# One strip for the last key tile of four heads, and values projected in 64-column pieces, in a fused cross-attention and expert-FFN kernel

## The reference

```
x = x + attention(layernorm(x), ctx)
x = x + experts(layernorm(x))
```

```
q = x @ Wq ;  k, v = split(concat(ctx, x) @ Wkv)
dots = q k^T * scale ;  masked where  key index > query index + 154
out = softmax(dots) v ;  out @ Wout + bout
```

## Time and profile before

| | |
|---|---|
| median of three runs | 375.83 us (374.93 to 376.63) |
| the profiled execution, its own time | 376.98 us |
| its span, first to last instruction | 375.2 us |
| PE busy | 352.5 us (94%), 4336 matmuls |
| ACT busy | 266.3 us (71%), 385 instructions |
| DVE busy | 211.8 us (56%), 724 instructions |
| POOL busy | 117.9 us (31%), 178 instructions |
| mean granted clock of PE | 0.971 of 2.4 GHz |

### The profile page before, as it was taken

The page is one execution under the profiler, slowest core; times in us unless marked ns, Lnnn a source line. Parts: engine busy times, 40 slices in busy tenths (PEclk is TensorE's granted clock), DMA queues, the critical chain, the costliest instruction groups (busy, mean ns, idle before and its releaser), DMA issues.

```text
span 375.2 us, 10982 instructions
## 1 busy us (share of the span) xinstructions
PE 352.5 (94%) x4336; PEld 228.0 (61%) x4336; DVE 211.8 (56%) x724; ACT 266.3 (71%) x385; POOL 117.9 (31%) x178
## 2 busy tenths in 40 slices
PE   8999999899999999999999999996858999999993
PEld 7757547343544444443534445585747899999992
DVE  4999698353637455563737445398778332323231
ACT  2675563899999999999999999614871545454630
POOL 5445775000004030300304030601431646464522
PEclk9999999899999999999999999999795999999999
DMA  7733799500538435553449513800660522322100
GB/s 245 199 111 116 247 238 312 183 6 3 140 108 271 122 101 139 155 140 96 119 130 260 126 36 63 279 0 2 224 226 3 146 88 65 106 73 92 59 26 31
DMA packets 37325, 47.68 MB, mean 127 GB/s; under 512 B 8764, under 2 KB 26610, under 8 KB 37265
## 3 DMA queue, kind: packets, MB, share of 16 engines
q1 hardware_dynamic: 34368, 40.26, 36.8%
q0 software_dynamic: 2560, 6.30, 5.6%
q10 hardware_dynamic: 337, 0.32, 0.3%
HBM read 32.71 MB, written 13.81 MB: 124 GB/s over the span
## 4 chain that ended last, share of the span: by engine, by line
PE 76%; DVE 10%; ACT 9%; issue 2%; POOL 2%; POOLq 0%
PE ps L1116 18%; PE ps L1092 16%; PE ps L1297 10%; PE ps L1309 9%; PE ps L1077 8%; ACT pbuf L858 8%; PE ps L1029 5%; DVE pbuf L1632 4%; PE ps L1230 3%; PE ps L999 1%; DVE stats L1666 1%; DVE xe L1661 1%; PE ps L1286 1%; PE ps L1178 1%; POOL pbuf L754 1%
## 5 line engine op out<-in xcount | busy, mean ns | idle before, releaser
L858 ACT ACTIVATE pbuf<-ps 128x1024 f32<-128x1024 f32 (+3 forms) x192 | 169.4, 1028 | 3.2 <-PE ps L1092 3.0
L1632 DVE SCALAR_TENSOR_TENSOR pbuf<-pbuf,seen 128x128 f32<-128x128 f32 (+2 forms) x288 | 76.4, 307 | 65.5 <-ACT pbuf L858 64.5
L1092 PE MATMUL ps<-q_st,k_st 98*32 98x512 bf16 (+4 forms) x2048 | 102.0, 319 | 2.8 <-ACT pbuf L858 2.6
L1116 PE MATMUL ps<-pbuf,v_st 128*32 128x512 f32 (+4 forms) x1024 | 98.0, 478 | 1.9 <-DVE pbuf L1632 1.9
L1092 PEld LDWEIGHTS ps<-q_st,k_st 98*32 98x32 bf16 x2048 | 51.8, 96 | 69.8 <-issue 28.1
L726 POOL TENSOR_TENSOR mid<-mid 64x256 f32<-64x256 f32 x28 | 20.5, 763 | 120.9 <-DMA mid<-reciprocals 120.9
L1116 PEld LDWEIGHTS ps<-pbuf,v_st 128*32 128x32 f32 x1024 | 27.5, 110 | 26.9 <-issue 11.8
L1297 PEld LDWEIGHTS ps<-mid,piece_f 128*128 128x128 f32 x320 | 38.7, 192 | 1.6 <-issue 0.7
L1297 PE MATMUL ps<-mid,piece_f 128*128 128x128 f32 x320 | 39.0, 275 | 0.5 <-issue 0.5
L1309 PE MATMUL ps<-pbuf,mid 128*128 128x256 f32 x160 | 37.7, 380 | 0.0
L940 ACT ACTIVATE mid<-ps 128x512 f32<-128x512 f32 x20 | 11.9, 597 | 34.4 <-PE ps L1297 34.3
(11 more groups left out here) (253 smaller groups left out, 370.2 us busy)
## 6 DMA issues: line engine op xcount, KB each, us to landing
wts<-in_L_ffn_W SPq DMA_DIRECT2D x16, 512.0 KB, 5.0
k_st<-k_cut SPq DMA_DIRECT2D x48, 147.2 KB, 3.0
q_st<-q_cut SPq DMA_DIRECT2D x48, 128.0 KB, 2.9
q_cut<-wts SPq DMA_DIRECT2D x8, 384.0 KB, 3.4
k_cut<-wts SPq DMA_DIRECT2D x8, 384.0 KB, 3.9
token_rows<-xe SPq DMA_DIRECT2D x4, 512.0 KB, 4.2
mid<-mid SPq DMA_DIRECT2D x28, 64.0 KB, 2.6
mid<-reciprocals SPq DMA_DIRECT2D x28, 64.0 KB, 2.3
```

The source lines that it names most:

```text
L858: nc.scalar.activation(pbuf[:, s % 2, r, c0:c1], st_ps[(s * GH + r) % NST][:, c0:c1], ACT.Exp, scale=SCALE).then_inc(exp_done, 1)
L1092: last = nc.tensor.matmul(st_ps[(s * GH + r) % NST][c:c + 32, a:z], k_st[pa][:, r, t * P + c:t * P + c + 32], q_st[pa][:, r, q0 + a - c0:q ...
L1116: last = nc.tensor.matmul(o_ps[32 * r:32 * r + 32, a:z], v_st[pa][:, t, r, :], pbuf[:, s % 2, r, a + dc:z + dc], start=(t == 0), stop=(t = ...
L1632: last = nc.vector.scalar_tensor_tensor(a, a, 3.0e38, seen[:, off:off + w], ALU.min, ALU.mult)
```

## The change

Tile 9 of the four heads shares one strip of `pbuf` and of PSUM. Head `h`'s 26 keys take the partitions 32h to 32h+25 of the tile's 26 columns in the slot of head 3. So

- `scores` leaves tile 9 out for heads 0 to 2 and makes for head 3 four matmuls, one for each head's keys and queries, one in each column group;
- `exps` ends 26 columns earlier (948 instead of 974) for heads 0 to 2 in step 3;
- `masks` handles tile 9 once, for head 3, with a mask `seen_short` that holds the corner of `seen` four times, one below the other, made by four more copies in `order_constants`;
- `values` reads the strip for all four heads. `v_st` of tile 9 keeps 128 rows, and head r's columns are zero outside its 32 rows; the column of ones is set by four small memsets a buffer instead of one;
- the value job that holds tile 9 projects the tile's first 32 rows (26 keys and 6 of padding) into each of the four partition groups, with the 64 columns of one head of each group of heads, so eight matmuls of 64 columns stand for two of 256;
- `load_v` makes four small copies of 32 rows by 16 columns, each waited for, then the copy of the nine other tiles, waited for too. Ahead of piece 15 it also waits for `low_done` of the pieces before.

```diff
--- before.py
+++ after.py
@@ -107,6 +107,9 @@
 
 
 LAST = NB * NG - 1
+SHORT = JT - 1
+SHORT_KEYS = J - SHORT * P
+assert SHORT_KEYS <= 32 and GH == 4 and any(len(tiles) > 1 and tiles[-1] == SHORT for tiles in STEP_TILES)
 
 
 def xattn_ffn(nc, x, ctx, Wq, Wkv, Wout, bout, Wg, W1, W2, out, rows_d, qd, kd, sums_d, recs_d, force_shift=False):
@@ -208,6 +211,7 @@
         before = sb("before", [P, P], BF16)
         ones_b = sb("ones_b", [P, P], BF16)
         seen = sb("seen", [P, P])
+        seen_short = sb("seen_short", [P, 32])
         irow = sb("irow", [P, 1], I32)
         ir2 = sb("ir2", [P, 1], I32)
         fcol = sb("fcol", [P, P])
@@ -281,6 +285,7 @@
         ones_rows = sem("ones_rows")
         rows_sent = sem("rows_sent")
         v_in = sem("v_in")
+        short_in = sem("short_in")
         biased = sem("biased")
         st_ready = sem("st_ready")
         exp_done = sem("exp_done")
@@ -687,8 +692,9 @@
                 made += 1
             pool.wait_ge(st_made, made)
             for i in range(2):
-                nc.gpsimd.memset(v_st[i][0:J - (JT - 1) * P, JT - 1, :, HD:HD + 1], 1.0).then_inc(st_made, 1)
-                made += 1
+                for r in range(GH):
+                    nc.gpsimd.memset(v_st[i][32 * r:32 * r + SHORT_KEYS, SHORT, r, HD:HD + 1], 1.0).then_inc(st_made, 1)
+                    made += 1
             pool.wait_ge(st_made, made)
             nc.gpsimd.memset(tri[:, :], 0.0).then_inc(tri_made, 1)
             pool.wait_ge(tri_made, 1)
@@ -697,15 +703,21 @@
 
             def load_v(pa, b, m):
                 g = 2 * m + pa
-                nc.gpsimd.tensor_copy(v_st[pa][:, :, :, 0:HD],
-                                      v_all[:, bass.ds(b, 1), :, bass.ds(g * (GH * HD), GH * HD)]
-                                      .rearrange("p b t (h c) -> p (b t) h c", h=GH)).then_inc(v_in, 1)
+                for r in range(GH):
+                    nc.gpsimd.tensor_copy(v_st[pa][32 * r:32 * r + 32, SHORT, r, 0:HD],
+                                          v_all[32 * r:32 * r + 32, b, SHORT, (g * GH + r) * HD:(g * GH + r + 1) * HD]).then_inc(short_in, 1)
+                    pool.wait_ge(short_in, (b * NG + g) * GH + r + 1)
+                nc.gpsimd.tensor_copy(v_st[pa][:, 0:SHORT, :, 0:HD],
+                                      v_all[:, b, 0:SHORT, g * (GH * HD):(g + 1) * (GH * HD)]
+                                      .rearrange("p t (h c) -> p t h c", h=GH)).then_inc(v_in, 1)
+                pool.wait_ge(v_in, b * NG + g + 1)
 
 
             for i in range(len(QK)):
                 w = JOBS[QK[i]][4]
                 if i == PER_B + 5:
                     pool.wait_ge(vcopy_done, len(VJ) // 2)
+                    pool.wait_ge(low_done, i)
                     for pa in range(2):
                         load_v(pa, 0, 0)
                 pool.wait_ge(lo_done, i + 1)
@@ -851,11 +863,12 @@
                     c0 = STEPS[s][0][2]
                     c1 = STEPS[s][-1][2] + S - STEPS[s][-1][1]
                     for r in range(GH):
+                        end = c1 - SHORT_KEYS if STEPS[s][-1][0] == SHORT and r < GH - 1 else c1
                         act.wait_ge(st_ready, (g0 * NSTEP + s) * GH + r + 1)
                         if r == 0:
 
                             act.wait_ge(pv_done, g0 * NSTEP + s + 1)
-                        nc.scalar.activation(pbuf[:, s % 2, r, c0:c1], st_ps[(s * GH + r) % NST][:, c0:c1], ACT.Exp,
+                        nc.scalar.activation(pbuf[:, s % 2, r, c0:end], st_ps[(s * GH + r) % NST][:, c0:end], ACT.Exp,
                                              scale=SCALE).then_inc(exp_done, 1)
 
             for g in range(2 * NG):
@@ -1026,8 +1039,15 @@
                     pe.wait_ge(tr_done, flipped(b, (t + 2) * P))
                     for i in range(2):
                         for k in range(KT):
-                            last = nc.tensor.matmul(bk[:, i * D:(i + 1) * D], xcT[:, b, k, (t + i) * P:(t + i + 1) * P],
-                                                    wkv_sb[:, k, D:2 * D], start=(k == 0), stop=(k == KT - 1))
+                            if t + i < SHORT:
+                                last = nc.tensor.matmul(bk[:, i * D:(i + 1) * D], xcT[:, b, k, (t + i) * P:(t + i + 1) * P],
+                                                        wkv_sb[:, k, D:2 * D], start=(k == 0), stop=(k == KT - 1))
+                                continue
+                            for r in range(GH):
+                                mine = bk[32 * r:32 * r + 32, i * D:(i + 1) * D].rearrange("p (g h c) -> p g h c", g=NG, h=GH)
+                                w_ap = wkv_sb[:, k, D:2 * D].rearrange("p (g h c) -> p g h c", g=NG, h=GH)
+                                last = nc.tensor.matmul(mine[:, :, r, :], xcT[:, b, k, SHORT * P:SHORT * P + 32], w_ap[:, :, r, :],
+                                                        start=(k == 0), stop=(k == KT - 1), skip_group_check=True)
                 elif job[0] == "s":
                     pe.wait_ge(w2_small, 48)
                     pe.wait_ge(mean_made, 2)
@@ -1087,6 +1107,12 @@
 
                 pe.wait_ge(exp_done, (g0 * NSTEP + s) * GH + r + 1)
                 for (t, q0, c0) in STEPS[s]:
+                    if t == SHORT:
+                        for h in range(GH if r == GH - 1 else 0):
+                            last = nc.tensor.matmul(st_ps[(s * GH + r) % NST][32 * h:32 * h + 32, c0:c0 + SHORT_KEYS],
+                                                    k_st[pa][:, h, t * P:t * P + 32], q_st[pa][:, h, q0:S],
+                                                    start=True, stop=True, skip_group_check=True)
+                        continue
                     for (a, z) in split_at_bank(c0, c0 + S - q0):
                         for c in range(0, P, 32):
                             last = nc.tensor.matmul(st_ps[(s * GH + r) % NST][c:c + 32, a:z],
@@ -1114,7 +1140,7 @@
                 for (t, a, z, dc) in pieces:
                     for r in range(GH):
                         last = nc.tensor.matmul(o_ps[32 * r:32 * r + 32, a:z], v_st[pa][:, t, r, :],
-                                                pbuf[:, s % 2, r, a + dc:z + dc],
+                                                pbuf[:, s % 2, GH - 1 if t == SHORT else r, a + dc:z + dc],
                                                 start=(t == 0), stop=(t == STEP_TILES[-1][-1]), skip_group_check=True)
                 if half == 1:
                     last.then_inc(pv_done, 1)
@@ -1460,6 +1486,8 @@
                 seq(nc.vector.tensor_scalar(before[:, :], fcol[:, :], frow[:, 0:1], None, ALU.is_gt))
                 seq(nc.vector.tensor_tensor(prev_e[:, :], before[:, :], same_e[:, :], ALU.mult))
                 seq(nc.vector.tensor_scalar(seen[:, :], fcol[:, :], frow[:, 0:1], None, ALU.is_ge))
+                for r in range(GH):
+                    seq(nc.vector.tensor_copy(seen_short[32 * r:32 * r + 32, :], seen[0:32, 0:32]))
 
             def digit_constants():
                 for half in range(2):
@@ -1624,6 +1652,11 @@
                     for r in range(GH):
                         v.wait_ge(exp_done, (g0 * NSTEP + s) * GH + r + 1 + NST)
                         for (t, q0, c0) in STEPS[s]:
+                            if t == SHORT:
+                                if r == GH - 1:
+                                    a = pbuf[:, s % 2, r, c0:c0 + SHORT_KEYS]
+                                    last = nc.vector.scalar_tensor_tensor(a, a, 3.0e38, seen_short[:, 0:SHORT_KEYS], ALU.min, ALU.mult)
+                                continue
                             w = min(P, S - q0)
                             off = 0
                             if t == 1:
```

## The result

The changed kernel takes 376.94 us in the median (375.22 to 378.14, 22 runs), the kernel before beside it 376.12 (374.43 to 378.00, 22 runs): a ratio of 1.0024, 95% interval 1.0012 to 1.0035. That is 0.9 us slower, where I had forecast 0.4 faster. The profiled execution has a span of 375.5 us at a mean granted clock of 0.968 and took 377.31 in all; before it was 375.2 at 0.971 and 376.98. Measured once more, the same pair gave 376.93 against 375.52, and the kernel before against itself 0.9993 (0.9978 to 1.0008). The difference is small, but the interval doesn't hold 1: it can be told from none.

What follows compares the result with a forecast made beforehand. ACT's exponentials were taken to set the attention's pace, PE nearly as full. -0.6 (ACT) - 0.6 (gaps) + 0.8 (start) = -0.4 us on the median of 375.83 gave 375.4 us, range 373.8 to 377.5.

Steps and rivals of the forecast that it cites:

- first rival: Ahead of the scores: the pieces' pipeline takes over the start, PE waits for `low_done`; +1.4, 377.2 us, chance 0.23.
- The forecast's own bound: Start of attention: forecast wrong if the first exponential comes earlier than 65.6 or later than 67.5; expected near 66.6.
- the slack: Between POOL's end at 63.89 and PE's arrival at 64.9: 1.0 us that hides DVE's added +0.8.
- the term of +0.8 for the start: DVE and POOL ahead of the scores: +0.8 net of PE's gain, bounds -0.8 to +2.2.
- (a): DVE's `order_constants`: four waited copies of 32 columns, about 0.2 each, delay piece 17 by +0.8.
- (b): POOL's two early `load_v`: +2.0 to +3.4 for both, about +2 hidden by POOL's 2.06 us wait before piece 17.
- (c): DVE instructions ahead of the scores, held beside POOL's pieces 15 and 16: 0 to +1.2.
- the case of the rule that I had named: DVE copies sharing ports with POOL: if all four were held, the start would be nearer the +2.2.
- PE's half value job: PE's projections: 16 short matmuls replace tile 9's half of 0.87; -0.4, twice, at most -0.8.
- The exponentials: ACT in the attention: 24 exponentials 26 columns shorter, 25 ns each, called sure: -0.6.
- The three gaps: ACT's idle 0.40 before groups 2, 4 and 6: -0.6 taken, 0.3 from shorter scores; bounds -1.2 to +1.2.
- The attention stage is 1.2 shorter: Sign to look for: 24 exponentials at 948 columns and 0.2 to 0.6 us less idle time before the 974-column ones.

Runs made afterwards that it cites:

- last job at full width: Changed kernel, with tile 9's half of the value job projected as before, two matmuls of 256 columns at full width: 376.41 us against 375.37, ratio 1.0026.
- flag early: Changed kernel, with the load of the flag into PE's register ahead of job `n` instead of `o`: 376.06 us against 375.33, ratio 1.0033.
- short matmuls first: Changed kernel, with tile 9's 16 short matmuls first in their value job, tile 8's four full-width ones behind: 376.53 us against 375.64, ratio 1.0020.
- three moves: Changed kernel, with `seen_short` copies before group 0's masks, early `load_v` behind all POOL pieces, flag's load ahead of `n`: 374.12 us against 375.33, ratio 0.9967.
- three moves, short first: Changed kernel, copies before group 0's masks, early `load_v` behind all pieces, flag's load ahead of `n`, tile 9's short matmuls first: 374.47 us against 375.64, 0.9973.
- moves without the strip: Kernel before, with the two early `load_v` behind all POOL pieces and the flag's load ahead of job `n`: 375.07 us against 375.52, ratio 0.9990.
- copies moved: Changed kernel, with the four copies into `seen_short` made before group 0's masks instead of in `order_constants`: 375.72 us against 375.37, ratio 1.0029.
- `load_v` moved: Changed kernel, with the two early `load_v` after all 20 POOL pieces instead of ahead of piece 15: 375.90 us against 375.37, ratio 1.0022.
- copies alone, no strip: Kernel before, with only the four copies into `seen_short` added to `order_constants`, read by nobody: 376.68 us against 375.37, ratio 1.0041.
- `load_v` alone, no strip: Kernel before, with `load_v` split into four small waited copies and one large, early ones also waiting for `low_done`: 376.22 us against 375.33, ratio 1.0028.
- reductions: Changed kernel, with the four copies into `seen_short` written as maxima over an axis of length 1, at their old place: 376.17 us against 375.33, 1.0033.
- the kernel that filled PE's waits: Kernel before, with five matmuls of ones behind the scores of three heads in the first group: 375.41 us against 375.52, ratio 0.9996.

## Why the prediction was wrong

Its first rival came nearest, to which I had given 0.23: "POOL's longer `load_v` and DVE's added copies hold each other from 50 us on, the last `low_done` comes after 66 instead of 63.89". It came at 66.25. But the rival's other half, PE waiting for `low_done`, did not happen: the first scores start 1.68 us after it. The forecast's own bound failed with it: a first exponential "later than 67.5" (68.60, and 67.79 in the second profile).

**The step that failed** is the slack: "+0.8 at DVE is +0.8 at the last `low_done`, 64.7, where PE now arrives at 64.9: only the 1.0 us of slack between 63.89 and 64.9 hides it". I let PE arrive on its own and meet `low_done` there. But waits on DVE stand on the way. The two value jobs ahead of `n` already waited 1.30 us until piece 17 had freed a bank (60.08 + 0.68, and PE at 60.82; at 59.15 before). The job `n` waits for DVE's last maxima: before they ended at 62.11 + 0.33 = 62.44, and `n` started at 62.60; after they ended at 64.80, and `n` started 0.14 later at 64.94, with PE idle for 0.40. With that 0.14 `n` had 0.02 us to spare. DVE's and PE's rows for it in the kernel before:

```profile
62.11 0.33 DVE L1484 TENSOR_REDUCE bpeak<-n 128x1 f32<-128x2 f32 x4
62.60 0.34 PE L1065 MATMUL ps<-bpeak,heads 128*128 128x4 f32 x2
```

And `o` waits for `over_done`, whose two-column product lasts until POOL's piece ends (0.73 us to 63.90 before, to 66.26 after; I had used the row only as an example of a hold). The same product takes 0.16 us at 49.5, with nothing beside it to hold it, and it ends with POOL's last piece in every row of the table. So this wait is tied to POOL's end too, by way of DVE. These are the steps from `n` on, read from the PE and DVE timelines of eight profiles, in us:

| kernel | n to over_done | n to o | o to scores | n to scores | over_done to scores |
|---|---|---|---|---|---|
| before | 1.52 | 2.11 | 0.41 | 2.52 | 1.00 |
| after | 1.53 | 2.24 | 0.75 | 2.99 | 1.46 |
| last job at full width | 1.53 | 2.12 | 0.41 | 2.53 | 1.00 |
| flag early | 1.53 | 1.67 | 0.74 | 2.41 | 0.88 |
| short matmuls first | 1.52 | 1.87 | 0.75 | 2.62 | 1.10 |
| three moves | 1.24 | 1.43 | 0.70 | 2.13 | 0.89 |
| three moves, short first | 1.24 | 1.63 | 0.50 | 2.13 | 0.89 |
| moves without the strip | 1.25 | 2.05 | 0.21 | 2.26 | 1.01 |

The last column never goes below 0.88. If 0.88 is the least, as three different kernels suggest, the scores of the kernel before, at 1.00, had 0.12 us to spare on this path, and 0.02 on that of `n`; either way the 1.0 us of my slack didn't exist, and +0.82 at piece 17 gave +0.88 at the first exponential when the copies stood alone. In the sum the term of +0.8 for the start measured +2.6: 0.8 of copies and 1.4 of holds, with no slack to hide them, and 0.47 more between `n` and the scores.

**The terms of the start.** (a) The four copies: 0.8 forecast, 0.79 measured free of POOL, right. (b) The two `load_v`: 1.97 + 2.1 = 4.06 us where 1.84 stood (51.09 to 55.15), +2.2, within +2.0 to +3.4, and hidden by POOL's wait as expected. (c) The holds, bounded by 0 to +1.2 and counted at the low end, since +0.8 net is already used up by the copies alone. They were `prev_e` 1.20 instead of 0.23, `seen` 0.52 instead of 0.29 and the copies 1.77 instead of 0.79, less 0.56 at `before`, which now escaped its hold: +1.6 by instruction (+1.4 counted from the `l` job, which itself ran 0.2 later), above the bound. POOL's pieces 15 and 16, a `load_v` later than before, lay beside the constants, and what met their 1.16 us instructions lasted about as long as those.

By the Trainium skill (SBUF — State Buffer, Who interferes with whom) a copy can take the shared ports, a product of two operands in SBUF contends with GpSimd's reads, and a `tensor_reduce` never contends on this chip. The runs agree in all three: 1.17 us for the fp32 copy, 1.20 for the product, 0.2 for the reduction in the same place. Of the four copies only the first was held, so the case of the rule that I had named, all four held and a start nearer the +2.2, is not what happened; the start moved by 2.6 all the same, not counting the projections' own lateness.

**PE's half value job.** Its size was right (0.43 us where 0.87 was reckoned, -0.4), the use of the second one wrong: I netted it against DVE's lateness. The first, near 37 us, did shorten its stretch, from 1.83 to 1.21 us between the start of its value job and the start of the next job (36.00 to 37.83 before, 36.86 to 38.07 after), and the later `l` job starts 0.35 sooner on average in the nine profiles with it (54.06) than in the seven without (54.41); but within the nine these starts lie up to 1.2 apart. The table has what it is worth: with the flag loaded early the scores follow `over_done` by the same 0.88, so that of the 0.4 only 0.11 reach them (2.52 to 2.41), 0.13 between the moves with and without the strip (2.26 to 2.13). As changed it costs +0.47. For the idle time before `o` the cause is shown: it is the flag's register load, which lost the full-width matmuls in front of it, for it disappears with the full width and it disappears with the early load. The rest, from `o` to the scores, goes back to 0.41 only with the full width. The branch stands there, but no run takes it apart, so that it is the branch is argued.

**What held.** The exponentials: -0.6 forecast, 0.7 to 1.0 measured. The three gaps: 1.2 before, 0.35 + 0.25 after, -0.6 as forecast; but the gaps behind the first group add up to 0 to 0.6 in the five other profiles without the strip and to 0 to 0.9 in those with it, so the strip can't be given the credit. "The attention stage is 1.2 shorter": leaving out the two profiles with the stall, it is 170.8 to 171.9 us (mean 171.2) in the four without the strip and 169.8 to 171.3 (mean 170.6) in the ten with it, so some 0.6; the 2.9 seen between the two first profiles have the stall in them. No run takes the memsets, the masks and the small weight loads apart.

**The sum that would have been right**: start +2.15 + 0.47 = +2.6, exponentials -0.7 to -1.0, hence +1.6 to +1.9. For every kernel the same sum is its own start, counted from the `l` job, and the exponentials where it has the strip (us, against the kernel before):

| kernel | start | sum | measured |
|---|---|---|---|
| after | +2.60 | +1.6 to +1.9 | +0.9 (0.5 to 1.3) |
| after, again | +2.61 | +1.6 to +1.9 | +1.5 (0.8 to 2.2) |
| copies moved | +1.77 | +0.8 to +1.1 | +1.1 (0.2 to 2.0) |
| `load_v` moved | +1.16 | +0.2 to +0.5 | +0.8 (0.0 to 1.7) |
| copies alone, no strip | +0.82 | +0.8 | +1.5 (0.7 to 2.3) |
| `load_v` alone, no strip | +1.36 | +1.4 | +1.1 (0.3 to 1.8) |
| last job at full width | +2.14 | +1.1 to +1.4 | +1.0 (0.3 to 1.7) |
| flag early | +2.03 | +1.0 to +1.3 | +1.2 (0.3 to 2.2) |
| reductions | +1.95 | +0.9 to +1.3 | +1.2 (0.2 to 2.3) |
| short matmuls first | +2.23 | +1.2 to +1.5 | +0.8 (0.1 to 1.4) |
| three moves | -0.39 | -1.4 to -1.1 | -1.2 (-2.0 to -0.4) |
| three moves, short first | -0.39 | -1.4 to -1.1 | -1.0 (-1.7 to -0.3) |
| moves without the strip | -0.27 | -0.3 | -0.4 (-1.0 to +0.2) |

Only the first row's sum lies wholly outside its interval, by 0.3 to 0.6 us, and this stays open. The stall of the first group, which both profiles of the kernel before have and none of the others, is a candidate by place and size (1.4 us of gaps); the kernel that filled PE's waits showed no gain from its absence, so this is argued, not shown. Two small terms are not in the sum and nearly cancel: the first half value job (-0.35, above), and the stretch behind the attention, which is 135.5 to 135.8 us in the six profiles without the strip and 135.7 to 136.6 in the ten with it (means 135.66 and 136.07). No run shows why; the granted clock there, 0.92 to 0.95 and 0.91 to 0.95, doesn't follow it.

## What to carry to other kernels

A slack between two engines is only as large as the smallest one on any wait between them: go through every wait that the consumer passes on its way, small jobs and two-column products too, before counting on it. When work is added or moved on POOL, go through what DVE does beside it one instruction at a time; each copy, product or conversion that starts beside a long POOL instruction can last as long as that, and on a chain of dependent ones this adds up. Shortening the matmuls in front of a register load brought nothing here: the load must be given cover, or moved to a place that has it.

## What the runs showed of the hardware

- An fp32 copy of 32x32 on DVE takes 0.2 us, and 1.17 when it starts beside a POOL instruction; a reduction with the same input and output is not held (four in 0.81 in the same place). A bf16 product of 128x128 goes from 0.23 to 1.20, and a 128x512 addition from 0.69 to 1.67, a product on two columns from 0.16 to 0.73. It works the other way too: four POOL copies of 32x16 take 2.55 us beside DVE's additions and 0.95 otherwise.
- PE's load of a register from SBUF costs 0.54 to 0.71 us of idle time in front of the next matmul when only short matmuls (16 in 0.43 us) stand before it, and nothing that shows behind eight in 1.96. From `o`, one column, to the scores behind the branch it is 0.41 us from start to start behind eight full-width matmuls, 0.21 when the register load is not between them either, and 0.50 to 0.75 in the kernels with the short ones; the time from DVE's result to the scores, through `o`, never fell below 0.88.
- Sixteen matmuls of 64 columns in four column groups, between full-width ones, take 0.43 us, 27 ns each; the whole job of them and four full-width ones takes 1.47 us, where eight full-width ones take 1.97, so that a cost for entering or leaving that tiling, if there is one, is small.
- A POOL copy of 32x16 takes 0.3 us with its own wait (four in 1.20 and 1.29).
